# One-hots and source masks of a graph-network kernel made per 128 columns with a scalar per partition, in place of one instruction on two tensors

## What is computed

```
h    = relu(layernorm(x))                    # 6250 x 64
e    = relu(concat(h[dst], edge_attr) @ W1.T + b1)
e    = relu(e @ W2.T + b2)                   # 206250 x 128
sum_, cnt = segment_sum(e, src), segment_sum(1, src)
agg  = sum_ / max(cnt, 1)
z    = relu(concat(h, agg, u) @ Wa.T + ba) @ Wb.T + bb
out  = x + z                                 # 6250 x 64
```

## Time and profile before

| what | value |
|---|---|
| median of 3 runs | 1947.66 us (1938.87 to 1948.65) |
| profiled execution, its own time | 1948.77 us |
| its span, first to last instruction | 1947.0 us |
| outside the span | 1.8 us |
| mean granted TensorE clock | 0.964 of full speed |
| busy, share of the span | PE 89%, PEld 76%, DVE 70%, ACT 59%, POOL 80% |
| DMA | 372 MB, 191 GB/s over the span |

### The profile page before, as it was taken

The page is one execution under the profiler, slowest core; times in us unless marked ns, Lnnn a source line. Parts: engine busy times, 40 slices in busy tenths (PEclk is TensorE's granted clock), DMA queues, the critical chain, the costliest instruction groups (busy, mean ns, idle before and its releaser), DMA issues.

```text
span 1947.0 us, 42075 instructions
## 1 busy us (share of the span) xinstructions
PE 1733.4 (89%) x12472; PEld 1471.2 (76%) x12472; DVE 1363.0 (70%) x3557; ACT 1146.0 (59%) x2542; POOL 1553.5 (80%) x991
## 2 busy tenths in 40 slices
PE   5798788999999999999998999999999999977917
PEld 3577677787888788877877887888888888866815
DVE  8567566677777777777776777877776777744618
ACT  4476666666666666666566666666666666642303
POOL 8388888888888888888888888888888888888850
PEclk9899999999999999999999999999999999998959
DMA  9888888999999999999999999999999999998756
GB/s 349 222 165 163 144 152 147 180 193 196 199 197 189 199 195 194 194 194 190 192 189 189 195 199 186 206 192 194 200 188 201 196 202 193 198 202 175 159 119 206
DMA packets 322272, 372.04 MB, mean 191 GB/s; under 512 B 42592, under 2 KB 203584, under 8 KB 321408
## 3 DMA queue, kind: packets, MB, share of 16 engines
q1 hardware_dynamic: 185856, 306.18, 55.7%
q0 software_dynamic: 135360, 62.15, 34.2%
q10 hardware_dynamic: 832, 0.97, 0.2%
HBM read 203.87 MB, written 159.27 MB: 187 GB/s over the span
## 4 chain that ended last, share of the span: by engine, by line
POOL 43%; issue 17%; PE 15%; DMA 12%; DVE 7%; SPq 4%; ACT 1%; POOLq 0%; DVEq 0%; ACTq 0%
POOL sums L811 38%; DMA sums<-regA,idx 7%; POOL sums L799 5%; PE bank L1326 4%; PE bank L1315 3%; PE bank L1363 3%; PE bank L1337 3%; DMA regC<-slots 2%; PE bank L1353 1%; DMA sums<-vscat,vidx 1%; SPq L585 1%; DVE regC L1193 1%; ACT regA L921 1%; DVE regC L1179 1%; DMA src<-rows_src 1%
## 5 line engine op out<-in xcount | busy, mean ns | idle before, releaser
L811 POOL DMA_INDIRECT sums<-regA,idx x844 | 1358.8, 1610 | 294.8 <-issue 241.9
L1315 PEld LDWEIGHTS bank<-h,regC 128*128 128x128 f32 x3072 | 389.7, 194 | 198.1 <-ACT h L933 164.1
L1315 PE MATMUL bank<-h,regC 128*128 128x130 f32 x3072 | 423.5, 281 | 76.6 <-ACT h L933 75.5
L1363 PE MATMUL bank<-w,h 128*128 128x128 f32 x3224 | 436.0, 279 | 0.0
L1337 PE MATMUL bank<-regA,L 128*128 128x512 f32 x806 | 426.2, 611 | 10.3 <-DVE regA L1112 4.6
L1363 PEld LDWEIGHTS bank<-w,h 128*128 128x128 f32 x3224 | 402.8, 196 | 0.8 <-issue 0.8
L913 ACT ACTIVATE h<-bank,b1c 128x512 f32<-128x512 f32 x403 | 274.8, 682 | 180.2 <-PE bank L1337 168.5
L921 ACT ACTIVATE regA<-bank 128x520 f32<-128x520 f32 x211 | 127.3, 603 | 402.0 <-DMA sums<-regA,idx 346.5
L1326 PE MATMUL bank<-regC 128*128 128x129 f32 x2352 | 301.1, 282 | 15.7 <-ACT vscat L944 8.2
L1353 PEld LDWEIGHTS bank<-h,regC 128*128 128x128 f32 x1688 | 225.0, 193 | 116.8 <-issue 98.2
L933 ACT ACTIVATE h<-bank 128x512 f32<-128x512 f32 x403 | 239.7, 595 | 111.4 <-PE bank L1363 109.5
(11 more groups left out here) (139 smaller groups left out, 1258.4 us busy)
## 6 DMA issues: line engine op xcount, KB each, us to landing
regC<-slots SPq DMA_DIRECT2D x294, 260.0 KB, 5.1
regA<-in_ea SPq DMA_DIRECT2D x202, 256.0 KB
slots<-regC SPq DMA_DIRECT2D x192, 260.0 KB
src<-rows_src SPq DMA_DIRECT2D x107, 256.0 KB
slots<-regC SPq DMA_DIRECT2D x192, 138.1 KB
sums<-regA,idx POOLq DMA_INDIRECT x844
dstR<-rows_dst SPq DMA_DIRECT2D x101, 128.0 KB
sums<-zeros SPq DMA_DIRECT2D x20, 645.0 KB, 8.4
```

The source lines that it names most:

```text
L811: nc.gpsimd.indirect_dma_start(out=sums[k], out_offset=bass.IndirectOffsetOnAxis(ap=idx[:, n % RING, t:t + 1], axis=0), in_=scat[:, n % 4, ...
L1315: last = T.matmul(psSlot(t)[:, k, :], place, h2[:, g % 2, t, :], start=True, stop=True)
L1363: last = T.matmul(psL2(g % 2)[:, t * H:(t + 1) * H], h1[:, g % 2, t * TILE:(t + 1) * TILE], w2[:, :], start=False, stop=True, skip_group_c ...
```

## The change

In both places the one instruction over 4 tiles becomes 4 instructions of 128 columns. Each takes one tensor from SBUF and a scalar per partition (the column of srcF, or the key at the end of the loaded row). In the second, the bin's number is a constant: lows less key is compared with -b, in place of key less b with lows. The semaphores are raised by the last of the instructions. Waits, buffers, data types and the order of everything else stay.

```diff
@@ -1144,8 +1144,9 @@
                     m = ROW_PAIR_OF[g]
                     dve.wait_ge(sB_in[m % 2], 16 * (m // 2 + 1))
                     wait(dve, sum_done, n - 3)
-                    VE.tensor_tensor(S[:, n % 4, :, :], sB_of(g).rearrange("p (t e) -> p t e", t=TPG), srcF[:, TPG * g:TPG * (g + 1)].unsqueeze(2).broadcast_to([P, TPG, TILE]),
-                                     ALU.is_equal).then_inc(mask_ready, 1)
+                    for t in range(TPG):
+                        made = VE.tensor_scalar(S[:, n % 4, t, :], sB_of(g)[:, t * TILE:(t + 1) * TILE], srcF[:, TPG * g + t:TPG * g + t + 1], None, ALU.is_equal)
+                    made.then_inc(mask_ready, 1)
                 if is_plain(s - 3):
                     n = PLAIN_NO[s - 3]
                     dve.wait_ge(scat_ready, n + 1)
@@ -1176,8 +1177,8 @@
                     dve.wait_ge(unit_in[buffer_of(m)], 16 * arrived(m))
                     wait(dve, unit_done, m - 1)
                     for i in range(nb):
-                        made = VE.scalar_tensor_tensor(out=oh2[0:rows, m % 2, i, :, :], in0=loaded(m)[0:rows, i, :, C:W].broadcast_to([rows, TPG, LO]), scalar=-float(b),
-                                                       in1=lows[0:rows, i, :].unsqueeze(1).broadcast_to([rows, TPG, LO]), op0=ALU.add, op1=ALU.is_equal)
+                        for t in range(TPG):
+                            made = VE.tensor_scalar(oh2[0:rows, m % 2, i, t, :], lows[0:rows, i, :], loaded(m)[0:rows, i, t, C:W], -float(b), ALU.subtract, ALU.is_equal)
                     made.then_inc(oh2_ready, 1)
                 if s == XBB_STEP:
                     dve.wait_ge(wz_in, 16 * 5)
```

## The result

| | before | after |
|---|---|---|
| median of 16 runs | 1945.05 us (1938.87 to 1953.68) | 1933.09 us (1927.89 to 1951.83) |
| ratio | | 0.9932, 95% interval 0.9916 to 0.9949 |
| span of the profiled execution | 1947.0 us | 1938.7 us |

What follows compares the result with a forecast made beforehand. GpSimd's back-to-back scatters were taken to set the pace. From the profiled 1948.8 us, minus 5 (before 360 us), minus 26 (even stage), plus 7 (tail) gave 1924.8, forecast as 1924 us, range 1904 to 1962.

Steps and rivals of the forecast that it cites:

- The mechanism of the gain: Scatters starting under L1147 or L1179 wait until its stream ends; 182 lost 44.5 us, net gain 38 us.
- The price of one instruction: On VectorE, one new instruction takes 281 ns, 0.20 us from start to start; each replacement adds 0.19 us.
- waits on GpSimd: VectorE's new instructions wait for what GpSimd holds: 0.1 us a group of four, 50 us in all.
- what is late next: Even stage: TensorE's waits at L1387 for VectorE grow by 10 us, so 26 of 31 us are gained.
- The tail: Up to 1833 us, VectorE's added time lies on the path: 0.75 us a round, nine rounds, +7 us.
- the wide range: Whole kernel: time between 1904 and 1962 us, with 0.1 beyond the high end and 0.05 below the low end.
- the likeliest case: Whole kernel: the forecast of 1924 us, 1.2% faster, with its own range 1908 to 1938; chance 0.55.
- Another bound takes over: Rival: another engine bounds the even stage, which gives back only 10 us, 1940 us, or less, 1945; chance 0.2.
- GpSimd is held longer: Rival: four new instructions hold scatters without a gap, 96 us lost in place of 44.5; 2007 or 1981 us; chance 0.09.
- VectorE comes late to TensorE: Rival: at L1387 and L1326 VectorE's added time reaches TensorE, 50 us lost; 1968 us, or 1955 to 1960; chance 0.11.
- The slow rate: Rival: the new instructions stream at the two-tensor rate, 0.47 us more per replacement; 1937 us; chance 0.05.

Runs made afterwards that it cites:

- split_two_tensor: Kernel before, with L1147 and L1179 each cut into four 128-column instructions that keep two tensors in SBUF: 1935.24 us, ratio 0.9952 to the kernel before.
- the two halves: Kernel before with only L1147 made per 128 columns, 1934.42 us (0.9954), and with only L1179 made so, 1938.11 us (0.9971).
- after_relieved: Changed kernel with VectorE's L1121 cut from 49 bins to 8 from the third binned group on: 1934.57 us, ratio 0.9947 to the kernel before.
- before_relieved: Kernel before with VectorE's L1121 cut from 49 bins to 8 from the third binned group on: 1944.19 us, ratio 0.9996 to the kernel before.
- units_only: Kernel before with only the one-hots of the units (L1179) made per 128 columns: 1938.11 us, ratio 0.9971 to the kernel before.

## Why the prediction was right and where it was wrong

**The mechanism of the gain was right.** It was read from three places of the timeline and counted over the trace, and split_two_tensor and the two halves bear it out: a scatter that starts under a VectorE instruction with two SBUF inputs gets going when that instruction's stream ends. The trace before has two more signs of it. It isn't the length that counts: L1121 takes 975 ns and has one of its two inputs in PSUM ("bank"), and the 65 scatters that start well inside it lose 0.001 us on average. And the instruction must have started a little ahead of the scatter: an L1179 that starts up to 0.031 us ahead of the scatter doesn't hold it, one that starts 0.038 us ahead holds it for 0.52 us. 31 us came off the scatters where the sum said 38. The new instructions themselves hold them little (some 80 scatters, 4 us in all, by the same rule of 0.13 us). The missing 7 us lie with L1112, whose 512 columns on one tensor delayed 99 scatters by 13 us, where it was 47 and 6.

**The price of one instruction was right.** 281 ns forecast, medians of 281 (L1181) and 285 (L1148) measured, and 0.196 us from start to start for 0.20. For waits on GpSimd I took 50 us. VectorE's busy time rose by 1478.6 - 1363.0 = 115.6 us where 96 + 50 were forecast, so the waits came to some 20.

**The step that failed** is the one on what is late next: "I take -26 us of the 31." In the profiled execution the stage gave 4, with 25 us off its scatters; 21 became free time of GpSimd. The prediction named the next limit in the right place: TensorE at L1388 behind VectorE, 22.0 us on the matmul and 26.1 on the weight load before, 56.5 and 74.8 after, and most of GpSimd's new free time follows such waits. But I priced it by VectorE's added work, at 10 us, and that was the wrong cause: after_relieved takes 106 us of work away and gains nothing. VectorE is late because it waits in its order for loads that land just in time: with the stores off SP's queue those waits and TensorE's at L1388 go together. Both loads had rows before the change: L1179 and L1147 with 66.7 and 58.0 us behind DMAs. I read them as idle time of an engine with time to spare. They hardly grew with the change (111.6 to 120.2 us in the even stage, where TensorE's two waits went from 48 to 131), so a late load isn't new. Why TensorE's waits grew isn't shown, and as before_relieved has them at no cost, their total isn't their price.

**The tail was a second wrong term,** and the two errors partly cancelled. 0.75 us a round were forecast. Before, a round took 7.3 us; after, the next run of L1181 starts 8.06 us later (1781.48 and 1789.54 us). That is right, but "+7 us" didn't come: from the 869th scatter to the last it took 136.7 us before and 136.2 after. The prediction had the path wrong there. The chain after goes through GpSimd and the landings of its scatters from 1740 us on, and the last scatter starts at 1868.8 us, 11.0 before that of the kernel before. In all, the 8.3 us between the two traces are 1.6 ahead of the first scatter, 4.8 up to the 150th, 4.1 to the 869th, 0.5 in the tail, and 2.7 lost after the last scatter, where the sum had 5, 26 and -7.

**Luck and limits.** The measured 1933 us lies in the wide range and also in the likeliest case's own, 1908 to 1938. With the tail's term at nothing, the forecast would have been 1917, 16 us from the result, so part of the nearness is luck. The bound "less than 0.5% can't be told from no change" was too careful: with 16 runs a side the interval is 0.17% to either side, and units_only's 0.3% is clear of it.

**The rivals.** "Another bound takes over" was the nearest to what happened, and it took more than half of the gain. Its candidates were TensorE and the DMA engines, and neither was tested by itself. "GpSimd is held longer" is refuted by the 31 us. "VectorE comes late to TensorE" happened as a wait and not as a loss below the old time. The slow rate didn't come.

The Trainium skill, "SBUF — State Buffer", section "Who interferes with whom", infers that a tensor_tensor leaves descriptor generation alone. The traces disagree: L1185 at 910.93 us keeps a scatter for 3.1 us. By that inference the time would have risen after the change, and it fell. The same section also states that a VectorE instruction with two SBUF inputs contends with a GpSimd instruction that reads SBUF, so the inference alone is what the traces speak against. What a scatter wants 0.13 us after its start isn't shown.

**What stays open.** In every version TensorE is busy for 1297 to 1314 of the 1380 us of the even stage, and the DMA engines at 0.93 to 0.95. Relief of VectorE, of single loads and of SP's queue each showed the next wait and no gain. That fits a loop in which TensorE, GpSimd with the landings of its scatters, and the DMA engines with SP's loads all need almost the same time, and whose queues then take turns in waiting. Relief of TensorE, of the DMA engines, or of the scatters' landings together with SP's queue, wasn't tried, so which one would have to give first isn't shown. No version here beat the changed kernel.

## What to carry to other kernels

On the engine that sets the pace read the length of single instructions, and look at what runs beside the long ones: a VectorE instruction with two tensors in SBUF can hold a scatter for as long as it streams, and cutting it into shorter ones costs VectorE a start each and gives the scatter its gap. Before counting on such a gain, look at what each engine that would be next waits for, not at how much time it has: loads that land just in time made VectorE late at 81% busy in the even stage. To see afterwards where a gain went, add up the engine that set the pace (its work, its usual gaps, its free time), since long waits elsewhere can cost nothing. And compare stages over more than one trace where the times differ by less than 1%. Here 12 of 31 us arrived.

## What the runs showed that was not expected

- At 128 columns a tensor_scalar with a scalar per partition costs the same as an instruction on two tensors: 0.196 against 0.201 us from start to start, though it streams twice as fast (0.51 against 1.06 ns a column). The scalar's 63 ns eat the 70 ns that the stream saves.
- One 3200-column instruction on two tensors stopped a scatter for 3.1 us. It runs once here; in a loop it would be dear.
- VectorE's instructions on one tensor wait in their turn, mostly those that start 0.4 to 0.8 us after a scatter: L1181 took up to 614 ns where it needs 281. The split form on two tensors has a mean of 284 to 286, so it hardly waits.
